# A Mamba block with a ternary feed-forward: stores of products on SyncE, D u on TensorE, the gate on VectorE, and layer-norm sums from ScalarE

## The chip, the cores and the metric

The kernel runs on one core of a Trainium2 chip. The time is device microseconds of one execution. The kernel before takes 3103.6 us (median of 3 runs, 3101.23 to 3104.07). The profiler sees the engines PE (TensorE), DVE (VectorE), ACT (ScalarE), POOL (GpSimd) and SP (SyncE, which only issues DMAs); in the listings, a name with q stands for an engine's queue of instructions that aren't counted as work.

## The reference, cut to what matters

The input x is 4 x 2048 x 256. A Mamba block, then a layer norm of the sum, then a gated feed-forward and another layer norm:

```
x, z   = split(hidden @ in_proj.T)             # 512 channels each
u      = silu(causal_conv4(x) + conv_b)
dt,B,C = split(u @ x_proj.T)                   # 64, 16, 16
delta  = softplus(dt @ dt_proj.T + dt_b)
h_t    = exp(delta_t A) h_{t-1} + (delta_t u_t) B_t     # 512 channels x 16 states
y_t    = sum_n h_t[n] C_t[n] + D u_t
x1     = layernorm(hidden + (y * silu(z)) @ out_proj.T)
f      = silu(s1 * x1 @ W1.T) * (s2 * x1 @ W2.T)        # 1024 wide, ternary weights
f      = gelu(sh1 * f @ H1.T);  f = gelu(sh2 * f @ H2.T)
out    = layernorm(x1 + s3 * f @ W3.T)
```

## The kernel before, in words

The work has two stages. The first runs the Mamba block over 16 tiles of 512 time steps (4 batch rows of 4 tiles), and computes the products W1 x1 and W2 x1 of each tile as well, which it stores to memory (`ab`). The second reads these products and does the rest of the feed-forward. The change touches the first stage; an opening tile without a scan stands ahead of its loop, and a closing part behind it.

**Groups and slots.** A tile has 512 x 16 recurrences of 512 steps. They go through VectorE in 64 groups of 128: 4 channel groups c of 128 channels, in each of them 4 quarters q of the 16 states, in each of these 4 blocks j of 32 channels. One `tensor_tensor_scan` does a group (L1267). Four groups with the same c and q are a step k, 0 to 15. All engines run through the same 64 slots a tile, each engine in its own order, with semaphores between them; in slot i the group n = 20 + i is scanned, so a tile's slots begin with its group 20 and end with group 19 of the next tile. What is done in which slot is written out by hand in tables at the top of the file.

**Who does what.** ScalarE makes exp(delta A) of each group into one of three PSUM banks, two groups ahead (`decay_of`, L908). The scan's other input, db = (delta u) B, comes from VectorE for three quarters (`times_b`, L1251) and from GpSimd for the fourth (L1129). GpSimd multiplies h by C (`times_c`, L1118) into one of two hc buffers. TensorE folds hc over the states into the bank p_y (`fold_step`, L650): four matmuls, one for each block of 32 channels, each with all 128 rows and 32 columns of the array; hc of step k can be written when the fold of k - 2 is done. When a channel group's 4 folds are done, VectorE computes u D + y from u and p_y (`skip`, L1291), and GpSimd multiplies by silu(z) (`gate`, L1146). TensorE then projects and adds the residual, ScalarE copies the four 128-row parts out (L919). For the norm, VectorE takes mean and variance in slots 1 to 5 (`bn_stats`, `bn_aggr`, L1301 and L1306), ScalarE gives a first 1/sqrt in slot 7, GpSimd refines it, ScalarE scales in slot 15.

**delta and its broadcasts.** For each channel group of the next tile, TensorE, ScalarE and VectorE compute the softplus; GpSimd finishes delta and delta u (L1137, L1141). SyncE then runs `copies(t, c)` (L418): it stores delta's rows, stores delta u's rows, waits until these have landed, and loads each of them four times, to the four state rows of 32 partitions: eight loads of 256 KB. SyncE's program per tile was, in this order: copies of group 3, the store of x1, the load of x, copies of the next tile's group 0, the load of xT, copies of groups 1 and 2.

**The products.** Each tile has 16 products e (`AB_PLACES`: slot and bank of each). TensorE makes product e in its slot, ScalarE copies it in the next slot to one of three buffers (`copy_product`, L972), for which the store of product e - 3 has to have landed, and issues the store another slot later (`store`, L957), after waiting for its own copy. After every second product it issues the load of a pair of weights (L951) into a ring of four.

Of the kernel before, what the change touches and what calls it, by code (L numbers as in the profile page):

```python
# [106 lines left out]
SKIP_AFTER, GATE_AFTER = GC - JC + FOLD_AFTER + 1, GC - JC + FOLD_AFTER + 3  # L107
# [3 lines left out]
LN_SLOT = 15  # L111
EXP_LEAD = 2

# [18 lines left out]
GATE_SLOT, FIRST_SLOT = 42, 51  # L132
# [62 lines left out]
def mamba_stage(nc, sems, flag, xT, x, in_wT, conv_w, conv_b, xp_wT, dt_wT, dt_b, A_log, D_param, out_wT,  # L195
                fold, spread, ident, w1T, w2T, h1T, h2T, w3T, scales, d_rows, du_rows, w12, x1, ab):
    ctx = ExitStack()
    with ctx:
# [44 lines left out]
        fold_w = sb("fold_w", [P, GD])  # L243
        taps = sb("taps", [P, KI, TAPS])
        cb = sb("cb", [P, KI])
        dtb = sb("dtb", [P, KI])
        dpar = sb("dpar", [P, KI])
# [3 lines left out]
        stats = sb("stats", [P, SUB, 6])  # L251
        mv = sb("mv", [P, SUB, 2])
        var4, y4, a4, nb4 = (sb(name, [P, SUB]) for name in ("var4", "y4", "a4", "nb4"))
# [62 lines left out]
        y_sb, gated = sem("y_sb"), sem("gated")  # L316
        ln_dve, ln_act, ln_pool, ln_out = sem("ln_dve"), sem("ln_act"), sem("ln_pool"), sem("ln_out")
# [52 lines left out]
        N_NEWTON = 7  # L370
# [14 lines left out]
        kept.stores += [(ab_out[k], PAST.count(ab_uses(k), ab_uses(k) + ABOUT0)) for k in range(ABRING)]  # L385

# [10 lines left out]
        def _(sp):  # L397
            for dst, src in (
                (w_in[:], in_wT.rearrange("(k p) e -> p k e", p=P)),
                (w_xp[:], xp_wT.rearrange("(k p) e -> p k e", p=P)),  # L400
                (w_dt[:], dt_wT),
                (w_out[:], out_wT.rearrange("(k p) e -> p k e", p=P)),
                (taps[:], conv_w.rearrange("(k p) w -> p k w", p=P)),
                (cb[:], conv_b),
                (dtb[:], dt_b),
                (dpar[:], D_param),
                (a_neg[:], A_log),
                (fold_w[:], fold),
                (db[:, 0, 0:2, :].rearrange("p a t -> p (a t)")[DTR:P], spread),
                (db[:, 1, 0, 0:P], ident),  # L410
            ):
                sp.dma_start(dst, src).then_inc(weights_in, 16)
# [5 lines left out]
            def copies(t, c):  # L418

                k = c % 2  # L420
                sp.wait_ge(delta, t.count(KI, c + 1))
                sp.dma_start(d_rows[k], sp_r[k][:]).then_inc(d_out[k], 16)
                sp.wait_ge(du, t.count(KI, c + 1))
                sp.dma_start(du_rows[k], sp_w[k][:]).then_inc(du_out[k], 16)

                sp.wait_ge(db_dve, t.count(KI * QV, QV * (c - 1) + DVE0))
                sp.sem_inc(waited, 1)
                sp.wait_ge(db_pool, t.count(KI, c - 1 + POOL0))
                sp.sem_inc(waited, 1)
                sp.wait_ge(du_out[k], t.count(32, 16 * (c // 2 + 1)))  # L430
                for nn in range(GN):
                    sp.dma_start(du_bc[k][nn * GD:(nn + 1) * GD, :, :],
                                 du_rows[k].rearrange("(j d) t -> d j t", d=GD)).then_inc(du_in[k], 16)

                sp.wait_ge(decay, t.count(NG, GC * (c - 1) + DECAY0))
                sp.sem_inc(waited, 1)
                sp.wait_ge(d_out[k], t.count(32, 16 * (c // 2 + 1)))
                for nn in range(GN):
                    sp.dma_start(d_bc[k][nn * GD:(nn + 1) * GD, :, :],
                                 d_rows[k].rearrange("(j d) t -> d j t", d=GD)).then_inc(d_in[k], 16)  # L440
# [27 lines left out]
            copies(OPENING, 0)  # L468
            load_next(OPENING)
            copies(OPENING, 1)  # L470
            copies(OPENING, 2)

            def tile(t):
                nxt = t.following()
                rows = slice(t.tt * NT, (t.tt + 1) * NT)
                if t is LAST_ROW[-1]:
                    closing_loads(t)
                copies(t, 3)
                store_x1(t)
# [5 lines left out]
                sp.dma_start(res[:], x[t.b, rows, :].rearrange("(s p) c -> p s c", p=P)).then_inc(x_in, 16)  # L485
                if exists(nxt):
                    copies(nxt, 0)
                if exists(nxt.following()):
                    load_next(nxt)
                if exists(nxt):  # L490
                    copies(nxt, 1)
                    copies(nxt, 2)
# [16 lines left out]
            def closing(t):  # L509
                for m in range(KH):  # L510
# [9 lines left out]
                sp.wait_ge(first_lo, KH)  # L520
                for j in range(RAW_PLACES + EARLY_POOL_PIECES):
# [10 lines left out]
            closing(LAST_ROW[-1])  # L532
# [3 lines left out]
        def _(pe):  # L536
# [268 lines left out]
        def _(act):  # L805
# [111 lines left out]
            def residual(t, s):  # L917
                act.wait_ge(out_mm, t.count(SUB, s + 1))
                act.activation(res[:, s, :], p_mm[s % 2][:, 0:DM], ACT.Copy).then_inc(out_sb, 1)  # L919

            def norm(t, i):
                if i == 7:
                    act.wait_ge(ln_dve, t.count(2 * SUB, 2 * SUB))
                    act.activation(var4[:], mv[:, :, 1:2].rearrange("p a b -> p (a b)"), ACT.Ln,
                                   bias=eps_col[:]).then_inc(ln_act, 1)
                    act.wait_ge(ln_act, t.count(2, 1))
# [23 lines left out]
            def load_w12(t, m):  # L950
                act.dma_start(w12_sb[m % W12RING][:].bitcast(F32), w12[m]).then_inc(w12_in[m % W12RING], 16)  # L951

            def store(t, e):
                at = (ab[0:TILES].rearrange("(b q) e p t -> b q e p t", q=TILES_B)[t.b, t.tt, e] if exists(t)
                      else ab[TILES, e])
                act.wait_ge(ab_sb, ab_done(t, e + 1))
                act.dma_start(at, ab_sbuf[e % ABRING][:]).then_inc(ab_out[e % ABRING], 16)  # L957

# [9 lines left out]
            def copy_product(t, e):  # L968
# [5 lines left out]
                m = e // 2 + W12RING  # L974
                if e % 2 == 1 and m < KH:
                    load_w12(t, m)
                elif e % 2 == 1 and exists(t):
                    load_w12(t.following(), m - KH)

# [6 lines left out]

            def ffn_stores(t, i):
                for e in range(AB):
                    if i == AB_PLACES[e][0] + 2:
                        store(t, e)  # L990
# [43 lines left out]
            def closing():  # L1034
                ffn_stores(PAST, 0)
                norm(PAST, LN_SLOT - 8)
# [11 lines left out]
                for e in range(AB):  # L1048
# [3 lines left out]
                    store(PAST, e)  # L1052
# [4 lines left out]
            def tile(t):  # L1057
                nxt = t.following()
                for i in range(NG):
# [3 lines left out]
                    if t is BEFORE and i == W12_FIRST:  # L1063
                        act.wait_ge(w12_out, 16 * 2 * KM)
                        for m in range(W12RING):
                            load_w12(OPENING, m)
                    if exists(t):
                        ffn_stores(t, i)
# [23 lines left out]
                if exists(t):  # L1092
                    ffn_stores(t, NG)
# [9 lines left out]
        def _(pool):  # L1103
# [4 lines left out]
            pool.sem_inc(gated, GATED0)  # L1108
# [34 lines left out]
            def gate(t, c):  # L1143
                pool.wait_ge(y_sb, t.count(KI, c + 1 + 1))
                pool.wait_ge(silu_z, t.count(1, 1))
                pool.tensor_tensor(z_of(t, c), u_of(t, c), z_of(t, c), ALU.mult).then_inc(gated, 1)  # L1146

            def norm(t):
# [5 lines left out]
                var = mv[:, :, 1:2].rearrange("p a b -> p (a b)")  # L1154
                mean = mv[:, :, 0:1].rearrange("p a b -> p (a b)")
                pool.wait_ge(ln_act, t.count(2, 2))
                pool.sem_inc(waited, 1)
                pool.tensor_scalar(var4[:], var, EPS, 1.0, ALU.add, ALU.mult).then_inc(ln_pool, 1)
# [8 lines left out]
                pool.tensor_tensor(nb4[:], mean, y4[:], ALU.mult).then_inc(ln_pool, 1)  # L1167
                done(6)
                pool.tensor_scalar(nb4[:], nb4[:], -1.0, 0.0, ALU.mult, ALU.add).then_inc(ln_pool, 1)

            def tile(t):
                nxt = t.following()
                for i in range(NG):
# [17 lines left out]
                    if n % GC == GATE_AFTER % GC:  # L1191
                        now, g = at_group(t, n - GATE_AFTER)
                        if exists(now):
                            gate(now, g // GC)
# [32 lines left out]
        def _(dve):  # L1227
# [4 lines left out]
            for j in range(KI):  # L1232
                for k in range(TAPS):
# [5 lines left out]
            dve.memset(res[:], 0.0).then_inc(out_sb, OUT0)  # L1239
# [3 lines left out]
            dve.sem_inc(y_sb, 1)  # L1243
# [50 lines left out]
            STATS_SLOT, AGGR_SLOT = 1, 5  # L1294

            def norm(t, i):
                if STATS_SLOT <= i < STATS_SLOT + SUB:
                    s = i - STATS_SLOT
                    if s == 0:
                        dve.wait_ge(out_sb, t.count(SUB, OUT0))  # L1300
                    dve.bn_stats(stats[:, s, :], res[:, s, :]).then_inc(ln_dve, 1)  # L1301
                elif i == AGGR_SLOT:
# [804 lines left out]
```

## Time and profile before

| what | us |
|---|---|
| median of 3 runs | 3103.6 |
| profiled execution | 3103.3 |
| its span, first to last instruction | 3101.5 |
| DVE busy | 2338.7 (75%) |
| PE busy | 2724.2 (88%) |
| ACT busy | 2010.8 (65%) |
| POOL busy | 1784.3 (58%) |
| one tile of the scan, the tenth of 16 | 117.7 |

The page gives the busy time of each engine over the span, and in 40 slices of it, about 78 us each. A group of instructions is printed with its line, engine, operation, result and operands, count, busy time and the mean duration of one, then the idle time of its engine just ahead of it and what ended that. A timeline row gives the start, the duration, the engine, the line and the operation, and in brackets the idle time ahead of it with its releaser. Durations of neighbours overlap a little, since instructions are pipelined; where it matters, differences of starts are taken.

### The profile page before, as it was taken

The page shows a single profiled execution, that of the slowest core. Times are in us where ns is not written, and L with a number is a line of the kernel's source. Part 1 is how long each engine was busy: PE and PEld are TensorE (multiplying, and loading weights), DVE is VectorE, ACT ScalarE, POOL GpSimd, SP SyncE. Part 2 cuts the span into 40 slices and gives each one's busy share as a digit, 9 for nine tenths or more (in the row PEclk, how much of TensorE's full clock was granted, in tenths as well). Part 3 has the DMA queues.
Part 4 walks back from the last instruction along what each step waited for, and adds up shares of the span by engine and source line. Part 5 has one row for each costly group of instructions (what it writes and reads, how often), then busy time and mean ns, then how long its engine had stood idle before and what let it go on. Part 6 is the DMA issues. An engine that isn't in the chain of part 4 may idle for free. (4 is left out here: it accounts for less than half of the span.)

```text
span 3101.5 us, 39954 instructions
## 1 busy us (share of the span) xinstructions
PE 2724.2 (88%) x11028; PEld 1636.8 (53%) x11028; DVE 2338.7 (75%) x2781; ACT 2010.8 (65%) x3383; POOL 1784.3 (58%) x920
## 2 busy tenths in 40 slices
PE   5788988888888888888888876889999999999997
PEld 2243443343343333333333332678888888888886
DVE  5999999999999999999999999434444454444442
ACT  3777777777777777777777777555555445555442
POOL 3899999899899899999999999400000000000000
PEclk8888898989889889889889887899999999999999
DMA  7366466466475475564565566542222222222210
GB/s 254 93 189 166 121 192 163 117 190 164 118 194 149 131 197 134 145 195 127 155 183 130 164 166 192 199 159 87 83 68 88 74 68 87 89 68 83 80 41 15
DMA packets 239642, 411.98 MB, mean 133 GB/s; under 512 B 23264, under 2 KB 63456, under 8 KB 239456
## 3 DMA queue, kind: packets, MB, share of 16 engines
q1 hardware_dynamic: 175680, 297.67, 35.3%
q10 hardware_dynamic: 63776, 112.22, 11.2%
q8 instruction: 69, 1.13, 0.2%
q14 instruction: 117, 0.96, 0.1%
HBM read 285.55 MB, written 124.26 MB: 132 GB/s over the span
## 5 line engine op out<-in xcount | busy, mean ns | idle before, releaser
L1267 DVE TENSOR_TENSOR_SCAN h<-bank,state,db 128x512 f32<-128x512 f32 x1024 | 1252.5, 1266 | 70.9 <-ACT bank L908 37.5
L1118 POOL TENSOR_TENSOR hc<-h,c_rows 128x1024 f32<-128x1024 f32 x512 | 1202.0, 2378 | 15.3 <-DVE h L1267 10.4
L908 ACT ACTIVATE bank<-d_bc,a_neg 128x512 f32<-128x512 f32 x1024 | 692.8, 685 | 314.5 <-DVE h L1267 201.9
L1627 ACT ACTIVATE hring<-s_bank,sc 128x512 f32<-128x512 f32 x248 | 170.5, 688 | 488.9 <-PE s_bank L1560 488.5
L1560 PE MATMUL s_bank<-mid,h_r 128*128 128x512 f32 x2048 | 469.1, 390 | 4.6 <-DVEq L1654 4.6
L722 PE MATMUL bank<-x_t,w 128*128 128x512 f32 x1088 | 394.1, 492 | 55.8 <-ACT ab L972 46.9
L1251 DVE TENSOR_TENSOR db<-bank,du_bc 128x2048 f32<-128x2048 f32 x192 | 435.1, 2266 | 8.1 <-issue 7.8
L1560 PEld LDWEIGHTS s_bank<-mid,h_r 128*128 128x128 f32 x2048 | 385.8, 188 | 85.6 <-ACTq L1598 5.0
L1129 POOL TENSOR_TENSOR db<-du_bc,b_row 128x2048 f32<-128x2048 f32 x64 | 291.7, 4558 | 102.4 <-DVE h L1267 97.7
L629 PE MATMUL bank<-bc,w_spread 64*128 64x512 f32 x272 | 155.6, 581 | 217.7 <-DVE db L1251 214.5
L650 PE MATMUL bank<-hc,fold_w 128*32 128x512 f32 x2048 | 334.6, 731 | 8.6 <-DVE u L1291 5.0
L722 PEld LDWEIGHTS bank<-x_t,w 128*128 128x128 f32 x1088 | 220.4, 217 | 215.4 <-issue 102.7
L629 PEld LDWEIGHTS bank<-bc,w_spread 64*128 64x128 f32 x272 | 58.0, 215 | 396.4 <-DVE db L1251 275.8
L582 PE MATMUL bank<-xb,w_conv 128*128 128x512 f32 x512 | 254.2, 626 | 13.4 <-ACT uz L829 9.5
L972 ACT ACTIVATE ab<-bank 128x512 f32<-128x512 f32 x272 | 160.1, 588 | 122.3 <-PE bank L722 107.7
L1560 PE MATMUL s_bank<-s_end,h_r 128*128 128x512 f32 x1024 | 235.7, 391 | 0.0
L1685 DVE TENSOR_TENSOR mid<-hring,mid 128x512 fp32r<-128x512 f32 x120 | 81.5, 690 | 177.7 <-ACT mid L1630 177.7
L1560 PEld LDWEIGHTS s_bank<-s_end,h_r 128*128 128x128 f32 x1024 | 191.8, 188 | 41.4
L582 PEld LDWEIGHTS bank<-xb,w_conv 128*128 128x128 f32 x512 | 90.0, 192 | 162.8 <-issue 142.9
L1560 PE MATMUL s_bank<-first_lo,h_r 128*128 128x512 f32 x448 | 175.4, 391 | 0.0
L1560 PE MATMUL s_bank<-first_hi,h_r 128*128 128x512 f32 x448 | 175.3, 391 | 0.0
L1685 DVE TENSOR_TENSOR first_lo<-hring,first_hi 128x512 fp32r<-128x512 f32 x64 | 44.3, 692 | 147.3 <-ACT first_hi L1630 147.3
(143 smaller groups left out, 3698.1 us busy)
## 6 DMA issues: line engine op xcount, KB each, us to landing
ab<-ab ACTq DMA_DIRECT2D x272, 256.0 KB, 4.1
du_bc<-du_rows SPq DMA_DIRECT2D x256, 256.0 KB, 4.9
d_bc<-d_rows SPq DMA_DIRECT2D x256, 256.0 KB, 7.9
s_abr<-ab SPq DMA_DIRECT2D x120, 512.0 KB, 3.9
w<-w ACTq DMA_DIRECT2D x136, 256.0 KB, 3.9
d_rows<-sp_r SPq DMA_DIRECT2D x64, 256.0 KB, 2.0
du_rows<-sp_w SPq DMA_DIRECT2D x64, 256.0 KB, 2.0
x<-res SPq DMA_DIRECT2D x17, 512.0 KB, 8.9
```

Of the source, the lines that this page charges most:

```text
L582: last = pe.matmul(p_mm[j % 2][:], w_conv[:, c, k, :], xb[:, c, k:k + NT], start=k == 0, stop=k == TAPS - 1)
L629: pe.matmul(dst[:], spread_w[:, which, :], bc[t.tt % 2][DTR:P, :], start=True, stop=True).then_inc(done, 1)
L650: last = pe.matmul(p_y[GD * j:GD * j + GD, :], fold_w[:], hc[:, k % HCSTEPS, j, :], start=q == 0, stop=q == QN - 1, tile_position=(0, GD * j))
L722: last = pe.matmul(product_bank(t, e)[:], w12_sb[m % W12RING][:, which, k, :], x_t[j][:, k, :], start=k == 0 and j == 0, stop=k == KM - 1 ...
L908: act.activation(decays[DECAY_BANK[g]][:], d_bc[c % 2][:, j, :], ACT.Exp, scale=a_neg[:, g:g + 1]).then_inc(decay, 1)
L972: act.activation(ab_sbuf[e % ABRING][:], product_bank(t, e)[:], ACT.Copy, scale=-1.0).then_inc(ab_sb, 1)
L1118: pool.tensor_tensor(hc[:, k % HCSTEPS, at:at + HG], h[:, H_SLOT[k], at:at + HG], c_rows[:, q, :].unsqueeze(1).broadcast_to([P, HG, NT]), ...
L1129: pool.tensor_tensor(db[:, k % DBSTEPS], du_bc[c % 2][:], b_row[:].unsqueeze(1).broadcast_to([P, JC, NT]), ALU.mult).then_inc(db_pool, 1)
L1251: dve.tensor_tensor(db[:, k % DBSTEPS], p_b[:].unsqueeze(1).broadcast_to([P, JC, NT]), du_bc[c % 2][:], ALU.mult).then_inc(db_dve, 1)
L1267: dve.tensor_tensor_scan(h[:, H_SLOT[k], j, :], decays[DECAY_BANK[g]][:], db[:, k % DBSTEPS, j, :], state[:, g:g + 1], ALU.mult, ALU.add). ...
L1560: last = pe.matmul(p_h[m % HBANKS][:], hidden_weights(layer, k, m), ins[j][:, k, :], start=k == 0 and j == 0, stop=k == KH - 1 and j == pa ...
L1627: act.activation(hring[c % RING][:], p_h[m % HBANKS][:], ACT.Gelu, scale=sc[:, 2 + layer, m:m + 1]).then_inc(gelu, 1)
```

## The change

It has four parts, and what goes with them.

1. Mean and variance: ScalarE's copy of the residual sum (L919) also accumulates its sum; in slot 1 ScalarE makes the negative mean, in slots 2 to 5 the squares of the differences with an accumulated sum, in slot 7 the first 1/sqrt from these. VectorE's `bn_stats` and `bn_aggr` go. GpSimd's refinement has one small operation less.
2. The gate: VectorE multiplies p_y by silu(z) straight from PSUM, in the slot where `skip` stood. GpSimd's gate goes.
3. D u: a matrix w_skip (the fold matrix with rows scaled by D, made once) multiplies u on TensorE into p_y, four matmuls of 32 x 32 in front of one of the folds of each channel group: step 3 of group 0, 2 of group 1, 1 of groups 2 and 3.
4. The stores of the products and the loads of weights: SyncE issues them, in slots. Its whole program is put in slots for that: the four steps of `copies` in the slots 6 to 9 after that group's `DT_SLOTS`, the store of x1 in slot 17, the load of x in 23, of xT in 34, some loads of the closing part in 25, 29 and 38.

```diff
+GATE_AFTER = GC - JC + FOLD_AFTER + 1
+SKIP_STEP = (3, 2, 1, 1)
+COPY_AFTER, COPY_STEPS = 6, 4
+STORE_SLOT, X_SLOT, XT_SLOT = 17, 23, 34
...
+            def products(t, i):
+                for e in range(AB):
+                    if i == AB_PLACES[e][0] + 2:
+                        store(sp, t, e)
+                        m = e // 2 + W12RING
+                        if e % 2 == 1 and m < KH:
+                            load_w12(sp, t, m)
+                        elif e % 2 == 1 and exists(t):
+                            load_w12(sp, t.following(), m - KH)
...
+                for i in range(NG):
+                    if t is LAST_ROW[-1]:
+                        first_loads(t, i)
+                    products(t, i)
+                    for step in range(COPY_STEPS):
+                        for now, c in dt_places(t, i, COPY_AFTER + step):
+                            if exists(now):
+                                copies(now, c, step)
+                    if i == STORE_SLOT:
+                        store_x1(t)
+                    elif i == X_SLOT:
+                        load_x(t)
+                    elif i == XT_SLOT and exists(nxt.following()):
+                        load_next(nxt)
...
                 if q == 0:
-                    pe.wait_ge(y_sb, t.count(KI, c + 1))
+                    pe.wait_ge(gated, t.count(KI, c + GATED0))
+                if q == SKIP_STEP[c]:
+                    for j in range(JC):
+                        at = slice(GD * j, GD * j + GD)
+                        pe.matmul(p_y[at, :], w_skip[at, c, :], u_of(t, c)[at, :], start=False, stop=False,
+                                  tile_position=(GD * j, GD * j))
                 pe.wait_ge(hc_done, t.count(TURNS * NK, TURNS * (k + 1) + HC0))
...
-                act.activation(res[:, s, :], p_mm[s % 2][:, 0:DM], ACT.Copy).then_inc(out_sb, 1)
+                act.activation(res[:, s, :], p_mm[s % 2][:, 0:DM], ACT.Copy,
+                               accum_out=sums[:, s:s + 1]).then_inc(out_sb, 1)
...
+                if i == MEAN_SLOT:
+                    act.wait_ge(out_sb, t.count(SUB, OUT0))
+                    act.activation(mean4[:], sums[:], ACT.Copy, scale=-1.0 / DM).then_inc(ln_act, 1)
+                elif MEAN_SLOT < i <= MEAN_SLOT + SUB:
...
+                    act.activation(sp_e[:, s % 2 * DM:(s % 2 + 1) * DM], res[:, s, :], ACT.Square, bias=mean4[:, s:s + 1],
+                                   accum_out=squares[:, s:s + 1]).then_inc(ln_act, 1)
...
-            def skip(t, c):
-                u = u_of(t, c)
+            def gate(t, c):
                 dve.wait_ge(folded, t.count(NK, QN * (c + 1) + FOLDED0))
-                dve.scalar_tensor_tensor(out=u, in0=u, scalar=dpar[:, c:c + 1], in1=p_y[:],
-                                         op0=ALU.mult, op1=ALU.add).then_inc(y_sb, 1)
+                dve.wait_ge(silu_z, t.count(1, 1))
+                dve.tensor_tensor(z_of(t, c), p_y[:], z_of(t, c), ALU.mult).then_inc(gated, 1)
```

## Rows read from the trace of the kernel before

**Rows 1.** The page: VectorE's busy share in 40 slices, in tenths.
```profile
DVE  5999999999999999999999999434444454444442
```
**Rows 2.** Windows, one tile: length, busy per engine (instructions), granted clock, DMA share, GB/s.
```profile
1136.25:1253.97 117.72, 100.20 (x363) 44.64 (x363) 112.41 (x99) 88.78 (x157) 108.75 (x56) 0.89 0.59 157
```
**Rows 3.** Waits over the whole span: us in total, times, longest.
```profile
ACT bank L908 <- ACT ab L972: 87.0, 149, 0.9
...
DVE h L1267 <- ACT bank L908: 37.5, 49, 2.9
DVE h L1267 <- POOL hc L1118: 29.4, 19, 2.0
```
**Rows 4.** Groups by line: count, busy us, mean ns, idle ahead and its releaser.
```profile
L1146 POOL TENSOR_TENSOR uz<-uz 128x512 f32<-128x512 f32 x48 | 62.0, 1292 | 9.4 <-DVE uz L1291 9.4
L1291 DVE SCALAR_TENSOR_TENSOR uz<-uz,dpar,bank 128x512 f32<-128x512 f32 x48 | 35.3, 734 | 4.9 <-PE bank L650 4.3
L1301 DVE BATCH_NORM_STATS2 stats<-res 128x6 f32<-128x256 f32 x68 | 27.7, 411 | 16.3 <-ACT res L919 16.3
L1285 DVE TENSOR_TENSOR bc<-bank,bc 32x512 fp32r<-32x512 f32 x16 | 11.0, 691 | 0.7
```
**Rows 5.** Timeline of VectorE, slots 0 to 5 of a tile.
```profile
1058.85 0.42 DVE L1301 BATCH_NORM_STATS2 stats<-res 128x6 f32<-128x256 f32 x1
1059.18 1.27 DVE L1267 TENSOR_TENSOR_SCAN h<-bank,state,db 128x512 f32<-128x512 f32 x1
...
1061.38 1.28 DVE L1267 TENSOR_TENSOR_SCAN h<-bank,state,db 128x512 f32<-128x512 f32 x1 [0.61 <-ACT bank L908]
...
1066.24 0.35 DVE L1306 BATCH_NORM_AGGREGATE mv<-stats 128x2 f32<-128x6 f32 x4
1066.51 1.25 DVE L1267 TENSOR_TENSOR_SCAN h<-bank,state,db 128x512 f32<-128x512 f32 x1
```
**Rows 6.** Timeline of TensorE: fold 13 in slot 42, granted clock low.
```profile
1016.62 1.94 PE L650 MATMUL bank<-hc,fold_w 128*32 128x512 f32 x8
```
**Rows 7.** Timeline of GpSimd: times_c 15, behind fold 13.
```profile
1018.75 4.71 POOL L1118 TENSOR_TENSOR hc<-h,c_rows 128x1024 f32<-128x1024 f32 x2 [0.20 <-PE bank L650]
```
**Rows 8.** Timeline of SyncE: the copies of group 1.
```profile
1026.07 0.33 SPq L424 DMA_DIRECT2D du_rows<-sp_w  x1
1028.09 1.87 SPq L432 DMA_DIRECT2D du_bc<-du_rows  x4
1030.14 2.12 SPq L439 DMA_DIRECT2D d_bc<-d_rows  x4
```
**Rows 9.** DMA issues at 1062.6: the last of eight copies, KB, us to landing.
```profile
d_bc<-d_rows SPq DMA_DIRECT2D x1, 256.0 KB, 8.4
```
**Rows 10.** DMA issues from 1031.0 to 1031.2, amid the copies of group 1.
```profile
d_bc<-d_rows SPq DMA_DIRECT2D x1, 256.0 KB, 8.7
ab<-ab ACTq DMA_DIRECT2D x1, 256.0 KB, 8.8
```
**Rows 11.** Timeline of ScalarE: copy of product 14 in slot 53, decay of slot 56.
```profile
1037.29 0.58 ACT L972 ACTIVATE ab<-bank 128x512 f32<-128x512 f32 x1
...
1038.77 0.69 ACT L908 ACTIVATE bank<-d_bc,a_neg 128x512 f32<-128x512 f32 x1 [0.90 <-DVE h L1267]
```
**Rows 12.** Timeline of VectorE: the scans of slots 40 and 56.
```profile
1010.38 1.28 DVE L1267 TENSOR_TENSOR_SCAN h<-bank,state,db 128x512 f32<-128x512 f32 x1 [1.80 <-POOL hc L1118]
...
1039.76 1.28 DVE L1267 TENSOR_TENSOR_SCAN h<-bank,state,db 128x512 f32<-128x512 f32 x1 [1.03 <-POOL hc L1118]
```
**Rows 13.** Timeline of TensorE at full clock: one product in two passes; a fold.
```profile
1089.61 1.02 PE L596 MATMUL bank<-uz,w_xp 128*96 128x512 f32 x2
1090.56 1.06 PE L650 MATMUL bank<-hc,fold_w 128*32 128x512 f32 x8
```
**Rows 14.** Timeline of SyncE and ScalarE: copies of group 0, copy of product 5.
```profile
1113.38 1.74 SPq L432 DMA_DIRECT2D du_bc<-du_rows  x4
...
1121.99 0.58 ACT L972 ACTIVATE ab<-bank 128x512 f32<-128x512 f32 x1
```

More of the change, by code:

```diff
@@ L385, in mamba_stage, with load_w12, store @@
         kept.stores += [(ab_out[k], PAST.count(ab_uses(k), ab_uses(k) + ABOUT0)) for k in range(ABRING)]
+        def load_w12(eng, t, m):
+            if m >= W12RING or not is_first(t):
+                eng.wait_ge(ab_sb, ab_done(t, 2 * (m - W12RING) + 2))
+            eng.dma_start(w12_sb[m % W12RING][:].bitcast(F32), w12[m]).then_inc(w12_in[m % W12RING], 16)
+        def store(eng, t, e):
+            at = (ab[0:TILES].rearrange("(b q) e p t -> b q e p t", q=TILES_B)[t.b, t.tt, e] if exists(t)
+                  else ab[TILES, e])
+            eng.wait_ge(ab_sb, ab_done(t, e + 1))
+            eng.dma_start(at, ab_sbuf[e % ABRING][:]).then_inc(ab_out[e % ABRING], 16)
         block = ctx.enter_context(nc.Block())
@@ L416, in load_xT, with copies @@
                              .rearrange("(k p) t -> p k t", p=P)).then_inc(xT_in, 16)
-            def copies(t, c):
+            def copies(t, c, step):
                 k = c % 2
[L421 to L440, printed above, removed]
@@ new lines, in copies @@
+                if step == 0:
+                    sp.wait_ge(delta, t.count(KI, c + 1))
+                    sp.dma_start(d_rows[k], sp_r[k][:]).then_inc(d_out[k], 16)
+                elif step == 1:
+                    sp.wait_ge(du, t.count(KI, c + 1))
+                    sp.dma_start(du_rows[k], sp_w[k][:]).then_inc(du_out[k], 16)
+                elif step == 2:
+                    sp.wait_ge(db_dve, t.count(KI * QV, QV * (c - 1) + DVE0))
+                    sp.sem_inc(waited, 1)
+                    sp.wait_ge(db_pool, t.count(KI, c - 1 + POOL0))
+                    sp.sem_inc(waited, 1)
+                    sp.wait_ge(du_out[k], t.count(32, 16 * (c // 2 + 1)))
+                    for nn in range(GN):
+                        sp.dma_start(du_bc[k][nn * GD:(nn + 1) * GD, :, :],
+                                     du_rows[k].rearrange("(j d) t -> d j t", d=GD)).then_inc(du_in[k], 16)
+                else:
+                    sp.wait_ge(decay, t.count(NG, GC * (c - 1) + DECAY0))
+                    sp.sem_inc(waited, 1)
+                    sp.wait_ge(d_out[k], t.count(32, 16 * (c // 2 + 1)))
+                    for nn in range(GN):
+                        sp.dma_start(d_bc[k][nn * GD:(nn + 1) * GD, :, :],
+                                     d_rows[k].rearrange("(j d) t -> d j t", d=GD)).then_inc(d_in[k], 16)
@@ L467, in _, with load_x @@
             sp.wait_ge(checked, 8)
[L468 to L479, printed above, removed]
+            for c in range(KI - 1):
+                for step in range(COPY_STEPS):
+                    copies(OPENING, c, step)
+                if c == 0:
+                    load_next(OPENING)
+            def load_x(t):
                 sp.wait_ge(x1_out, t.count(16, 16))
@@ L484, in tile @@
                 sp.sem_inc(waited, 1)
[L485 to L492, printed above, removed]
+                sp.dma_start(res[:], x[t.b, t.tt * NT:(t.tt + 1) * NT, :].rearrange("(s p) c -> p s c", p=P))\
+                  .then_inc(x_in, 16)
+            def tile(t):
+                nxt = t.following()
+                if t is LAST_ROW[-1]:
+                    closing_loads(t)
+                for i in range(NG):
+                    if t is LAST_ROW[-1]:
+                        first_loads(t, i)
+                    products(t, i)
+                    for step in range(COPY_STEPS):
+                        for now, c in dt_places(t, i, COPY_AFTER + step):
[7 more added lines that the diff above has]
+                        load_next(nxt)
             def load_pool(j):
@@ L507, in closing_loads, with first_loads @@
                     load_piece(sp, raw[j][:], j).then_inc(raw_h1_in[j], 16)
-            def closing(t):
-                for m in range(KH):
+            def first_loads(t, i):
+                for m in FIRST_LOADS.get(i, ()):
                     if m == 2:
@@ L1034, in closing @@
             def closing():
-                ffn_stores(PAST, 0)
-                norm(PAST, LN_SLOT - 8)
+                for i in range(8):
+                    norm(PAST, i)
                 norm(PAST, LN_SLOT)
@@ L1051, in closing @@
                     copy_product(PAST, e)
-                    store(PAST, e)
+                    store(act, PAST, e)
+                    m = e // 2 + W12RING
+                    if e % 2 == 1 and m < KH:
+                        load_w12(act, PAST, m)
             for i in range(X_SLOTS[0], X_SLOTS[-1] + 2):
@@ L1166, in norm @@
                 done(5)
[L1167 to L1169 removed]
+                pool.tensor_tensor(nb4[:], mean4[:], y4[:], ALU.mult).then_inc(ln_pool, 1)
             def tile(t):
@@ L1286, in low_rows @@
                                   rows[DTR:DTR + 2 * NS, :].bitcast(F32), ALU.subtract).then_inc(xd_lo, 1)
-            def skip(t, c):
-                u = u_of(t, c)
+            def gate(t, c):
                 dve.wait_ge(folded, t.count(NK, QN * (c + 1) + FOLDED0))
-                dve.scalar_tensor_tensor(out=u, in0=u, scalar=dpar[:, c:c + 1], in1=p_y[:],
-                                         op0=ALU.mult, op1=ALU.add).then_inc(y_sb, 1)
[L1294 to L1302, printed above, removed]
-                    dve.wait_ge(ln_dve, t.count(2 * SUB, SUB))
-                    dve.sem_inc(waited, 1)
-                    for s in range(SUB):
-                        dve.bn_aggr(mv[:, s, :], stats[:, s, :]).then_inc(ln_dve, 1)
+                dve.wait_ge(silu_z, t.count(1, 1))
+                dve.tensor_tensor(z_of(t, c), p_y[:], z_of(t, c), ALU.mult).then_inc(gated, 1)
             def not_rounded(piece, raw, rounded):
@@ L1370, in tile @@
                         low_rows(nxt)
-                    if n % GC == SKIP_AFTER % GC:
-                        now, g = at_group(t, n - SKIP_AFTER)
+                    if n % GC == GATE_AFTER % GC:
+                        now, g = at_group(t, n - GATE_AFTER)
                         if exists(now):
-                            skip(now, g // GC)
+                            gate(now, g // GC)
                     if t is LAST_ROW[-1]:
@@ L1389, in _ @@
                 tile(t)
-            for i in range(AGGR_SLOT + 1):
-                norm(PAST, i)
             dve.wait_ge(counted, 1)
```

97 lines of the change are left out of this document (38 added, 59 removed).

## The prediction

> **What bounds the kernel now.** First the page's busy slices [rows 1]: the span has two parts. Over the first 26 of 40 slices, the Mamba scan, VectorE reads 9 throughout; then the feed-forward part, which the change doesn't touch, follows. So the question is what one tile of the scan costs. The windows view from one tile's first group to the next [rows 2] gives 117.7 us a tile, of it VectorE 112.4, GpSimd 108.8, TensorE 100.2, ScalarE 88.8. VectorE sets the pace, and some 5 us a tile are waits of VectorE. The waits view names them [rows 3]: its scans wait 37.5 us in all for ScalarE's decays and 29.4 us for GpSimd; and ScalarE itself loses 87 us of idle ahead of decays behind its own copies of products: it waits for a copy to end, issues the store, and only then goes on. So what VectorE sheds is worth its full time, and what makes a decay late is paid in full as soon as it exceeds these small waits.
>
> **Part 1: statistics leave VectorE.** In the first five slots of a tile stand four bn_stats and four bn_aggr. From start to start [rows 5] a bn_stats costs 1059.18 - 1058.85 = 0.33, the aggregates 1066.51 - 1066.24 = 0.27: 4 x 0.33 + 0.27 = 1.6 us a tile (the mean of 0.41 in [rows 4] counts an overlap with the scan). Two of the four lie ahead of a scan that waits 0.61 for a decay after the large silu; that gain holds only if ScalarE comes as much earlier there, and it does: its last store before that silu goes away (next part). In exchange ScalarE gets a mean and four squares of 256 columns in slots 1 to 5, and accumulators on its four copies of the projection. They hide behind the scans: a decay goes to one of three banks and waits for the scan three groups back, so ScalarE has idle time there once it has caught up. If that cover were gone, each would delay a decay by its own length, about the 0.41 of the bn_stats [rows 4], 2 us a tile. I take 0. After the last tile ScalarE does for the last norm what VectorE did, the same number of passes over the same columns: 0.
>
> **Part 2: the gate.** skip (0.73, [rows 4]) becomes the gate on VectorE, one tensor_tensor with an operand in PSUM; nearest row 0.69. 4 x 0.04 = 0.16 a tile gained. GpSimd's four gates of 1.29 go; it is not the engine that VectorE waits for most, and its wait ahead of slot 40 (1.80, [rows 12]) is made by times_b and times_c after scan 55, which stay. Parts 1 and 2: 1.75 x 16 tiles = 28 us less.
>
> **Part 3: D u on TensorE.** Per channel group four matmuls on 32 x 32 blocks of the array, 512 columns. The nearest row is the fold, four column blocks side by side: eight passes in 1.06 at full clock [rows 13], 1.94 at half clock [rows 6]; the granted clock is at its lower level around slot 42, after TensorE waited for VectorE. Lower bound 0 (TensorE idles there anyway), upper bound one after another: one 512-column product of two passes is 1.02 [rows 13], so 4.1 at full and 8.1 at half clock. I take the fold's own price, 1.9 at half clock: same shape of output, same columns. In three of the groups TensorE waits for VectorE soon after, and the 1.9 disappears. In the fourth it does not: the skip of group 3 stands right ahead of fold 13. Fold 13 frees the hc buffer for which GpSimd's times_c 15 waits now already (0.20, [rows 7]); behind times_c 15 GpSimd does delta and du of the next tile's group 1, and these release SyncE's copies. So those copies go out 1.9 us later.
>
> By the Trainium skill's page "TensorEngine Tiling (Array Packing)", section "Restrictions and Gotchas", different row tiles cannot access the same PSUM bank at one time. The four blocks here are different row tiles that all write p_y. The fold of the trace has column blocks only, so no row here shows which holds; by the rule the price would be the upper bound above, and that is rival C.
>
> **Part 4: the stores on SyncE.** ScalarE gets back its issue waits (87.0 / 149 = 0.58 a store, [rows 3]), which removes the two waits of VectorE at slots 54 and 56. But SyncE issues in one order, slot by slot: steps 2 and 3 of the copies of group 1 stand at slots 46 and 47, the store of product 11 at slot 48. Now ScalarE issues that store beside them. The path in one tile, from VectorE's slot 40 at 1010.38 [rows 12]:
> - du's rows are stored at 1026.07 and the eight broadcast copies begin when they have landed, at 1028.09 [rows 8]. New: 1028.09 + 1.9 = 1030.0.
> - SyncE needs 1030.14 + 2.12 - 1028.09 = 4.2 us to issue them; the store of product 11 comes behind, at about 1034.
> - Transfers land in the order of their issue, whatever queue: a store that ScalarE issued at 1031.06 amid such copies took 8.8 us, the copy beside it on SyncE 8.7 [rows 10]. Eight undisturbed copies: the last, issued 3.2 to 3.6 after the first, takes 8.4 [rows 9], so all are there 11.7 after the first issue; with 2 us of latency (1026.07 to 1028.09) that is 1.2 for each 256 KB. The store lands at 1030.0 + 11.7 + 1.2 = 1042.9.
> - The ring of products has three buffers. The copy of product 14 (now at 1037.29, [rows 11]) needs the buffer of product 11, so it waits until 1042.9. Behind it on ScalarE's queue is the decay of slot 56: 1042.9 + 0.58 + 0.69 [rows 11] + 0.1 = 1044.3, where VectorE scans at 1039.76 today [rows 12].
> That is +4.55 us a tile, the wait of 1.03 that goes already counted. The bounds: with a hidden skip 1.9 less, +2.65; if the store were in time, -1.5 (the waits at slots 54 and 56, the first of which comes from the same store issues). TensorE and GpSimd wait meanwhile and catch up; nothing on VectorE later than slot 56 waits on a clock of its own, so the delay stays.
>
> The same happens at group 0, milder: there the copies begin at 1113.38, the store of product 2 comes behind them, and the copy of product 5 stands at 1121.99 [rows 14]. At the old time it would land at 1113.4 + 11.7 + 1.2 = 1126.3, 4.3 late. GpSimd, without the two gates ahead of that delta (2 x 1.29, [rows 4]) and on a VectorE that comes 0.6 earlier, brings the copies forward by 2.0: 2.3 late. Of that 1.8 falls into VectorE's wait at slot 40 [rows 12]. I count +0.5 a tile, and against it 0.5 for the waits that VectorE has at a tile's end that the last store's issue causes: 0. What else SyncE now does in that order costs 0: the loads of w12 fill a ring of four, two products ahead of need; the store of product 0 stands behind the load of x, which waits for x1 to land, but its buffer is wanted eight slots later; the load of xT moves to slot 34 and is wanted at slot 47.
>
> **The sum.** 15 tiles have copies for a next tile. In two of them TensorE runs at full clock at slot 42, and the delay is about 3.5; 13 x 4.55 + 2 x 3.5 = 66. With the 28 gained: +38 us. Against the profiled execution, 3103.3 (its span 3101.5 and 1.8 around it), that is 3141; the median of the runs is 3103.6, the same within 0.01%. I say 3140.
>
> **The rivals.**
> A, faster: product 11 lands before 1037 and there is no wait. It decides at a landing within 3 us of its issue at 1034. For it: a store with nothing ahead of it lands in 2 us [rows 8]. Against it: [rows 10]. Then VectorE gains 28, and up to 1.0 a tile at slots 54 and 56, 15: 3103 - 43 = 3060. Chance 0.17.
> B, about the same: TensorE hides the skip (full clock, or its wait for VectorE at slot 45 takes it up before GpSimd notices). 15 x 2.65 - 28 = +12: 3115. For it: the bound of GpSimd is only 0.20 wide [rows 7]. Against it: the clock there is low in 13 of 15 tiles. Chance 0.13.
> C, slower still: the four blocks run one after another. 6.2 more in the path of slot 42 a tile: 15 x 10.7 - 28 = +133, and delays at slots 14 and 26 on top: 3236 and more. Against it: the fold's blocks run side by side. Chance 0.08.
> D, slower: at group 0 GpSimd is not earlier, and of the 4.3 only 1.8 are covered: 15 x 2.5 = 37 more, 3177. For it: GpSimd is within 4% of VectorE [rows 2]. Against it: the two gates are real work. Chance 0.12.
> The forecast, 3118 to 3165, has 0.50.
>
> **The numbers.** No change means within 0.2%, 6 us, about what can be told from the runs. Faster: A and 0.03 of B, 0.20. The same: 0.06 of B and 0.04 of the forecast's low edge, 0.10. Slower: the rest, 0.70. The range leaves out most of A (below 3085) and C: 3085 to 3190. The forecast's own range is 3118 to 3165.
>
> **What would show it.** Right: in the waits, ScalarE's copies of products wait for ab stores by some 60 us or more (a few us now), in slot 53 of each tile, and VectorE's scans wait longest for ScalarE's decays; a tile is near 120 us; bn_stats is gone and the gate is near 0.69; the skip's passes are near the fold's. Wrong: if a store issued behind eight copies lands in under 5 us, or product 14's copy is not held, the path of part 4 fails and the kernel is faster; if the skip's four blocks are far apart in time, it is C.

## The result, and the profile after

The changed kernel takes 3179.0 us (median of 4 runs, 3166.7 to 3192.1) where the kernel before takes 3103.8 on the same chip: ratio 1.0245, with a 95% interval of 1.0202 to 1.0287. The forecast was 3140. The direction held and the time lies inside the outer range of 3085 to 3190, but above the forecast's own range, 3118 to 3165: the loss of 75 us is twice the 37 forecast. The profiled execution is the longest of the four: 3192.1 us, its span 3190.3, 88.8 more than the span before. From the end of the last scan on both kernels take the same (1148.3 us, 1147.8 before), so all of it lies in the scan's stage.

Windows of two tiles of the changed kernel, columns as in [rows 2]:
```profile
1189.44:1308.37 118.93, 102.30 (x396) 44.11 (x395) 110.33 (x90) 89.86 (x171) 103.82 (x51) 0.93 0.58 155
569.10:695.27 126.17, 108.07 (x399) 46.81 (x395) 110.46 (x91) 89.43 (x171) 103.80 (x50) 0.88 0.54 147
```
VectorE's work fell from 112.41 to 110.4 a tile, GpSimd's from 108.75 to 103.8, and yet a tile is longer. There are two kinds of tiles now, of 119 to 122 and of 124 to 127 us, the long ones at a lower granted clock.

The waits over the whole span, which answer to [rows 3]:
```profile
ACT ab L1032 <- DMA ab<-ab: 164.9, 34, 8.6
POOL hc L1165 <- PE bank L706: 154.1, 45, 8.0
...
DVE h L1303 <- ACT bank L964: 140.8, 75, 7.1
...
PE bank L778 <- ACT ab L1032: 102.9, 37, 6.1
```
The same two waits for stores and for folds in the kernel before:
```profile
ACT ab L972 <- DMA ab<-ab: 9.6, 7, 2.5
...
POOL hc L1118 <- PE bank L650: 2.6, 9, 1.0
```
Of the changed kernel's lines the first and the third are the forecast's: ScalarE's copies wait for stores, and VectorE's scans for the decays behind these copies. The second is new: GpSimd's times_c waits 154 us for folds. Nothing in the prediction has it.

SyncE's timeline at the copies of group 0, against [rows 14], then at those of group 1, against [rows 8]; both in the same tile:
```profile
1158.86 0.34 SPq L405 DMA_DIRECT2D ab<-ab  x1
1159.25 0.45 SPq L399 DMA_DIRECT2D w<-w  x1
1159.75 0.43 SPq L446 DMA_DIRECT2D du_rows<-sp_w  x1
1163.20 1.74 SPq L455 DMA_DIRECT2D du_bc<-du_rows  x4
1165.13 1.73 SPq L463 DMA_DIRECT2D d_bc<-d_rows  x4
1167.12 0.97 SPq L405 DMA_DIRECT2D ab<-ab  x2
...
1196.40 0.32 SPq L446 DMA_DIRECT2D du_rows<-sp_w  x1
...
1198.47 1.74 SPq L455 DMA_DIRECT2D du_bc<-du_rows  x4
1200.39 1.73 SPq L463 DMA_DIRECT2D d_bc<-d_rows  x4
1202.40 0.36 SPq L405 DMA_DIRECT2D ab<-ab  x1
```
The stores of product 2 (1167.12) and of product 11 (1202.40) stand behind eight copies each. The first took this long from issue to landing (the second 8.3), against [rows 10]:
```profile
ab<-ab SPq DMA_DIRECT2D x1, 256.0 KB, 9.1
```
The copy issued just ahead of it took 9.3. So on SyncE's queue, too, the store landed when the copies ahead of it had. What it does downstream, first on ScalarE (copies of products 5 and 14, against [rows 11]):
```profile
1176.31 0.60 ACT L1032 ACTIVATE ab<-bank 128x512 f32<-128x512 f32 x1 [5.21 <-DMA ab<-ab]
...
1210.76 0.60 ACT L1032 ACTIVATE ab<-bank 128x512 f32<-128x512 f32 x1 [3.82 <-DMA ab<-ab]
```
and then on VectorE (slots 38, 40 and 56, against [rows 12]):
```profile
1177.61 2.46 DVE L1303 TENSOR_TENSOR_SCAN h<-bank,state,db 128x512 f32<-128x512 f32 x2 [3.48 <-ACT bank L964]
1180.62 1.28 DVE L1303 TENSOR_TENSOR_SCAN h<-bank,state,db 128x512 f32<-128x512 f32 x1 [0.56 <-POOL hc L1165]
...
1212.24 1.28 DVE L1303 TENSOR_TENSOR_SCAN h<-bank,state,db 128x512 f32<-128x512 f32 x1 [3.60 <-ACT bank L964]
```
That is a short tile. TensorE waits for the copy of product 5 before it can make product 6:
```profile
1176.96 2.08 PE L778 MATMUL bank<-x_t,w 128*128 128x512 f32 x4 [5.27 <-ACT ab L1032]
```
In a long tile TensorE comes late between the two stalls. Its granted clock from product 6 (behind the copy of product 5) to fold 13, in the short tile and in a long one (busy, clock, DMA share, GB/s):
```profile
1176.96:1188.80 11.84, 11.04 (x44) 0.85 0.41 141
554.14:570.98 16.84, 15.79 (x44) 0.54 0.40 144
```
The wait is 5.3 us in the short tile and 4.5 in the long one. Behind it TensorE runs at the lower of its two levels (1.2 and 2.4 GHz), for a few us in the one tile, over almost the whole stretch in the other. The same 44 matmuls end 5 us later, and GpSimd's times_c 15, which releases delta and the copies of group 1, shows it:
```profile
571.32 4.73 POOL L1165 TENSOR_TENSOR hc<-h,c_rows 128x1024 f32<-128x1024 f32 x2 [7.66 <-PE bank L706]
```
In this execution 7 of 15 tiles are long. In another one (3168.5 us) there were 4. At some 5 us a long tile, that is most of the 23.6 us between these two.

VectorE's gate by line, against `skip` of [rows 4]:
```profile
L1327 DVE TENSOR_TENSOR uz<-bank,uz 128x512 f32<-128x512 f32 x64 | 43.2, 675 | 1.6 <-PE bank L706 1.1
```

### The profile page after: what moved, and what is told of

Its sections match the earlier page's. It is cut to its first block and busy times, and to the rows that moved or that the text cites. A ratio compares the mean times of both kernels' runs of the same rounds, so it can differ in the third digit from the quotient of the medians.

```text
span 3190.3 us, 41089 instructions
## 1 busy us (share of the span) xinstructions
PE 2791.1 (87%) x11540; PEld 1648.6 (52%) x11540; DVE 2305.7 (72%) x2650; ACT 2030.7 (64%) x3600; POOL 1700.8 (53%) x839
## 5 line engine op out<-in xcount | busy, mean ns | idle before, releaser
L706 PE MATMUL bank<-hc,fold_w 128*32 128x512 f32 x2048 | 309.8, 681 | 5.9 <-DVE uz L1327 5.3
L679 PE MATMUL bank<-bc,w_spread 64*128 64x512 f32 x272 | 144.1, 541 | 177.4 <-DVE db L1287 177.4
```

Source lines behind the costliest of these rows:

```text
L679: pe.matmul(dst[:], spread_w[:, which, :], bc[t.tt % 2][DTR:P, :], start=True, stop=True).then_inc(done, 1)
L706: last = pe.matmul(p_y[GD * j:GD * j + GD, :], fold_w[:], hc[:, k % HCSTEPS, j, :], start=q == 0, stop=q == QN - 1, tile_position=(0, GD * j))
```

## The experiments

Times are medians; the kernel before had 3102 to 3105 beside them. **S** is the theory that the loss is two stores behind eight copies.

**Stores on ScalarE again.**
```diff
-                    products(t, i)
...
+                    if exists(t):
+                        ffn_stores(t, i)
```


> The changed kernel, but ScalarE issues the stores of the products and the loads of weights again, as before; SyncE's copies keep their new slots. Theory S (two stores wait behind the eight broadcast copies of groups 0 and 1): both stalls are gone, only parts 1 to 3 are left, 3103 - 28 = 3075 us (3065 to 3085), no wait of ScalarE's copies for ab stores over 20 us in all, and no wait of times_c for a fold. Rival T (the skip on TensorE, or the norm's passes on ScalarE, make the loss): the waits of times_c for folds stay, and the time stays above 3130.


Measured 3080.1 (ratio 0.9929, 0.9906 to 0.9951). Its waits:
```profile
POOL hc L1176 <- PE bank L705: 62.8, 31, 3.8
...
ACT ab L1031 <- DMA ab<-ab: 5.6, 6, 2.1
```
Parts 1 to 3, with SyncE's other work in slots, gain 24.6, the forecast's 28 nearly. The wait for stores is gone. That for folds is not, which S had wrong, but VectorE's scans wait no longer for GpSimd than before (23.6 us in all, 29.4 before). Moving the issue to SyncE makes the loss: 3179 - 3080 = 99.

**Copies behind the stores.** SyncE keeps all issues; only steps 2 and 3 of the copies of groups 0 and 1 (the loads, four in each step) move in its order.
```diff
-COPY_AFTER, COPY_STEPS = 6, 4
+COPY_PLACES, COPY_STEPS = ((6, 7, 10, 12), (6, 7, 10, 11), (6, 7, 8, 9), (6, 7, 8, 9)), 4
```


> The changed kernel, SyncE still issues everything, but steps 2 and 3 of the copies of group 0 stand behind the stores of products 2 and 3 (slots 30 and 32), those of group 1 behind the store of product 11 (slots 48 and 49). Theory S: both stalls go; ScalarE also keeps its gain from not issuing, so 3055 to 3080 us. Rival Q (a store issued by SyncE is late in itself, because one queue issues everything in turn): ScalarE still waits for ab stores by 80 us or more and the time is above 3120. Rival T: above 3130.


Measured 3059.0 (0.9854, 0.9831 to 0.9877). Its waits:
```profile
POOL hc L1166 <- PE bank L707: 51.5, 26, 4.6
...
ACT ab L1033 <- DMA ab<-ab: 10.6, 8, 3.8
```
So the order alone costs 120 us, and with the stores in time it is 21 better that SyncE issues them than that ScalarE does. This is rival A's state, and its 3060.

**One group at a time.** The same edit with (6, 7, 8, 9) kept for group 1, then for group 0.


> Only group 0's copies moved behind the stores of products 2 and 3; product 11 still behind eight copies. Theory S, with the group 0 stall as the cause of the long low clock of TensorE and so of the late fold 13 in some tiles: left is 15 x 3.1 us at slot 56, 3075 + 47 = 3122 us (3105 to 3130), delta of group 1 13 to 14 us after slot 40 in every tile, tiles all of one length. If the late fold 13 comes from the skip instead: some tiles still 5 us longer, 3140 or more.

> Only group 1's copies moved behind the store of product 11; product 2 still behind eight copies of group 0. Theory S: the stall at slot 38 and its sequel at slot 42 stay, some 3.3 us a tile or 50 us in all, the one at slot 56 goes: 3075 + 50 = 3125 us, up to 3150 where the late fold 13 of some tiles still makes group 1's decays late. If group 0's stall were taken up by GpSimd's slack at slot 40, as I had counted: 3075 to 3085.


Measured 3165.5 with group 1's stall alone, which no theory had, and 3118.5 with group 0's alone, as S. Against 3059 the stalls are worth 106 and 60, together 120: they overlap. My 47 for group 1 was too small since I took the 3.1 us by which slot 56 of a short tile is later than in the kernel before; without any stall that slot comes 1.5 earlier than before, and with group 0's stall gone TensorE is at its lower level at fold 13 in nearly all tiles. ScalarE's copy of product 14 with group 1's stall alone, and VectorE's scan behind it:
```profile
1305.79 0.60 ACT L1033 ACTIVATE ab<-bank 128x512 f32<-128x512 f32 x1 [6.72 <-DMA ab<-ab]
```
```profile
1307.27 1.28 DVE L1304 TENSOR_TENSOR_SCAN h<-bank,state,db 128x512 f32<-128x512 f32 x1 [6.01 <-ACT bank L965]
```
From slot 40 (1273.65) to that scan it is 33.6 us; the prediction had 1044.3 - 1010.38 = 33.9. In these tiles GpSimd begins delta of group 1 13.5 to 15 after slot 40; with group 0's stall alone 9 of 15 have it at 17 to 18.5. So the long tiles are a sequel of group 0's stall.

**Part 4 alone.** The kernel before with SyncE's program of the changed one.


> The kernel before with SyncE's new program alone: it issues the stores and the loads of weights in the changed kernel's slots; statistics, gate and D u stay where they were. Theory S: the loss lies here alone, and parts 1 to 3 only hide 24 us of it (3080 with them and ScalarE's stores, against 3105 before): 3179 + 24 = 3203 us (3185 to 3220), with ScalarE's copies of products 5 and 14 waiting for stores as in the changed kernel. Rival T (the new operations make part of the loss): well under that, 3150 or less.


Measured 3250.3 (1.0473, 1.0441 to 1.0504): part 4 by itself makes the loss, as S has it, but the loss is 146, above S's range, and parts 1 to 3 give back 71 of it, not 24. Delta of group 0 comes 1.6 us later than in the changed kernel (GpSimd still has the gates; that these make it was not tried by itself), its copies begin 15 to 17 us after slot 24 in place of 14, the copy of product 5 follows, and ScalarE waits longer:
```profile
ACT ab L1008 <- DMA ab<-ab: 191.1, 33, 7.9
```

**Part 1 alone.**


> The kernel before with the mean and variance from ScalarE's sums alone. By the forecast's count 1.6 x 16 = 26 us less than before, 3078, so that parts 2 and 3 with SyncE's other slots are worth 0 beside it (3080 was measured with all). If the squares on ScalarE delay decays in slots 2 to 5, 0.4 each: 3090 or more, and parts 2 and 3 give the rest.


Measured 3092.0, 12.5 less: half of the count. That is the time of the expectation's second reading, but not its reason: the scans of slots 3 to 7 wait for nothing. VectorE's timeline, slot 2, against the 0.61 of [rows 5]:
```profile
938.26 2.46 DVE L1277 TENSOR_TENSOR_SCAN h<-bank,state,db 128x512 f32<-128x512 f32 x2 [1.38 <-ACT bank L907]
```
VectorE loses 1.5 us of work a tile and gains 1.1 of waits, 0.7 of it here: the two bn_stats that stood ahead of this scan were cover. The prediction's condition, that ScalarE comes earlier there, does not hold while ScalarE issues the stores: the scans of slot 2 wait 20.9 us in all here and 21.1 with parts 1 to 3 and the stores on ScalarE, but 13.8 with SyncE issuing in time (9.5 before). The other 12 of the 24.6 were not taken apart.

**The skip's price.** In the kernel with group 1's stall, D u is left out.
```diff
-                    for j in range(JC):
+                    for j in range(0):
                         at = slice(GD * j, GD * j + GD)
                         pe.matmul(p_y[at, :], w_skip[at, c, :], ...
```


> The kernel with group 0's copies reordered (3165 us) without the matmuls of D u, which are left out of y. The forecast put the skip at 1.9 us at half clock in the path fold 13, times_c 15, delta, copies, store of product 11, copy 14, slot 56. If that holds: 15 x 1.0 to 1.9 less, 3137 to 3150. If TensorE's idle time hides the skip, or the copies wait for something else: 3160 to 3168.


Measured 3099.7, 66 less. TensorE with and without the skip, ahead of fold 13 at the lower level:
```profile
1279.89 1.93 PE L703 MATMUL bank<-uz,w_skip 32*32 32x512 f32 x8
1281.76 1.70 PE L707 MATMUL bank<-hc,fold_w 128*32 128x512 f32 x8
```
```profile
1248.59 2.07 PE L779 MATMUL bank<-x_t,w 128*128 128x512 f32 x4
1250.59 1.46 PE L707 MATMUL bank<-hc,fold_w 128*32 128x512 f32 x8
```
The skip takes 1.87, the 1.9 of the forecast, and slot 56 moves by 1.9 (31.6 after slot 40 in place of 33.6, over 15 tiles). As much again comes between slot 56 and the next tile's slot 24 (1.5 a tile), where VectorE's waits of slots 0 and 2 fall from 33 to 10 us in all; the forecast had put the skips of the other groups, which stand there, at nothing. Which of them makes it was not tried.

> The kernel with both groups reordered (3059 us) without the matmuls of D u, which are left out of y. In the kernel with group 1's stall the same removal gave 66 us. Theory P (the skip costs what the path through fold 13 and the copies makes of it): with no copy of a product waiting for a store, 0 to 10 us less, 3049 to 3059. Rival T (the skip costs by itself, wherever it stands): again some 60 less, about 3000.


Measured 3079.6: 21 us slower than with the skip; both theories miss. Windows from slot 44 to 52 of one tile, with the skip and without (columns as in [rows 2]):
```profile
1227.41:1241.81 14.40, 12.98 (x52) 6.20 (x49) 14.40 (x13) 10.77 (x23) 12.30 (x7) 1.00 0.54 162
```
```profile
1239.28:1254.77 15.49, 13.18 (x40) 5.94 (x41) 14.50 (x12) 10.19 (x21) 12.47 (x7) 0.78 0.57 169
```
With less to do TensorE is granted less (0.78 for 1.00) and needs longer for fewer matmuls. VectorE's gate at the end of that stretch then waits for the fold, 12.7 us in 15 tiles, and not at all with the skip:
```profile
1254.16 0.69 DVE L1328 TENSOR_TENSOR uz<-bank,uz 128x512 f32<-128x512 f32 x1 [0.99 <-PE bank L707]
```
The stretch from slot 40 to 56 is 1.3 longer a tile, 19 of the 21.

**TensorE kept busy in its wait.** The changed kernel, with extra matmuls whose result nobody reads; BUSY is 10 in the first run and 5 in the second.
```diff
+                if e == 6 and exists(t):
+                    pe.wait_ge(gated, t.count(KI, KI - 1 + GATED0))
+                    for _ in range(BUSY):
+                        pe.matmul(p_y[:], w_out[:, 0, 0:P], w_out[:, 0:2, :].rearrange(...), start=True, stop=True)
```


> The changed kernel (3179 us) with ten extra matmuls into p_y in each tile, ahead of TensorE's wait for the copy of product 5, at a time when p_y is free: 4 us of work in a wait of 5. Theory K (after that wait TensorE is granted its lower clock, for long in some tiles, and fold 13 is late for that): the clock stays up, no delta of group 1 later than 15 us after slot 40, tiles of one length near 120, 3145 to 3165. Rival B (fold 13 is late from the backlog of that wait alone): unchanged or later, 3175 to 3190.

> The changed kernel with five extra matmuls into p_y ahead of TensorE's wait for the copy of product 5, in place of ten: ten took 8.85 us there, 4 more than the wait, and the scan of slot 40 waited for that, 68 us in all against 8. Five take 4.4, inside the wait. Theory K (late fold 13 comes from the granted clock after that wait): tiles of one length near 120, no delta of group 1 later than 15 us after slot 40, the wait at slot 40 small again, 3145 to 3165. Rival B: two lengths of tiles as in the changed kernel, 3175 to 3190.

> The changed kernel itself beside the run above, on the same chip: 3165 to 3192 us, in steps of some 5 us for each tile with a late fold 13.


With ten: 3188.5, in B's range, but not for B's reason: all tiles are of one length (121 to 125) and delta of group 1 begins 12 to 13 after slot 40 in every tile, as K has it, while the extra work outlasts the wait. With five: 3123.7, beside 3169.6 for the changed kernel itself (3158 to 3188), 46 less. The stretch that was at 0.85 and 0.54 above, from product 6 to fold 13 (columns as in [rows 2]):
```profile
1139.50:1151.00 11.50, 10.16 (x46) 4.19 (x46) 10.11 (x9) 10.04 (x20) 9.03 (x5) 1.00 0.46 156
```
No tile is long any more (117 to 121). That is theory K, and more than its 3145 to 3165, since the short tiles also had a stretch at the lower level.

**The last tile.**
```diff
-FIRST_LOADS = {25: (0, 1), 29: (2, 3, 4, 5), 38: (6, 7)}
+FIRST_LOADS = {32: (0,), 33: (1,), 34: (2,), 35: (3,), 36: (4,), 37: (5,), 38: (6,), 39: (7,)}
...
-                    elif i == X_SLOT:
+                    elif i == (33 if t is LAST_ROW[-1] else X_SLOT):
```


> The kernel with both groups reordered (3059 us), and in the last tile the load of x after the store of product 3 (slot 33 in place of 23) and the eight loads of the next stage one a slot from slot 32 on. Its last tile took 37.9 us from slot 24 to the last scan against 33.8 before, with product 2's store issued 4.5 us later. Theory S (again stores behind something on SyncE's queue): 4 us less, 3055. If the last tile is held by the loads' traffic and not by the order: no difference.


Measured 3053.6 (0.9833, 0.9815 to 0.9851), 5.4 less, near S's 4; but in the profiles the last tile itself gives only 1.9 of that. The rest lies where nothing was changed, so it is not shown to be the edit's. It is the fastest version: 51 us below the kernel before.

## Why the prediction was wrong

The mechanism of part 4 was right, and group 1 came near its price; **the step that failed is group 0: "I count +0.5 a tile, and against it 0.5 ...: 0"**. The runs show +1.74 a tile there, 26 us, and a sequel in the next stretch that the sum does not have; as the only stall it costs 60 (3118.5 against 3059.0). By differences of scan starts, means over 15 tiles, profiled execution against profiled execution; the last column but one is the execution with 4 long tiles, and the forecast's 0 of group 0 stands as its two halves, 0.5 x 15 each, in the stretches where they belong:

| stretch | before | after | change x 15 | with 4 long tiles | forecast |
|---|---|---|---|---|---|
| slot 24 to 40 (group 0's stall) | 29.23 | 30.97 | +26 | +26 | +8 |
| slot 40 to 56 (group 1's) | 29.08 | 34.45 | +81 | +66 | +66 |
| slot 56 to 24 of the next tile | 59.11 | 57.53 | -24 | -33 | -34 |
| opening, last tile, closing | | | +6 | +6 | -2 |

Group 0's term is not the whole of it. Without that stall alone the kernel still takes 3165.5, not 3140. In its profile the first two stretches are then -3 and +67, but the third gains only 15 in place of 34; with D u left out as well it gains 38. So the skips that were put at nothing ("the 1.9 disappears") have a price in that kernel.

- **Parts 1 and 2**, -28: -24.6 with the stores on ScalarE. VectorE's work fell by 2.0 a tile, a little more than the 1.75 counted; bn_stats and bn_aggr are gone, the gate takes 0.675. Part 1 by itself loses half of its gain to the wait of slot 2.
- **Part 3**: the price of 1.9 at the lower level is right in the path of fold 13; for the other groups see above. Rival C is out. By the Trainium skill's page "TensorEngine Tiling (Array Packing)", section "Restrictions and Gotchas", different row tiles cannot access one PSUM bank at one time. Here four 32 x 32 blocks at four row tiles write p_y in 1.87 us, the time of the fold's column blocks at that level (1.94, [rows 6]), so the trace does not show that price.
- **Part 4, group 1**: copies at 1030.0, product 11's store issued at about 1034, landed at 1042.9, slot 56 at 1044.3; with this stall alone, counted from slot 40, they came 19.9, 23.8, 32.1 and 33.6 after it, where the forecast had 19.6, 23.6, 32.5 and 33.9. In the changed kernel the short tiles are earlier (31.6 to 33.0) since TensorE is back at full clock at fold 13, and the seven long ones later (35.4 to 37.6). In the execution with 4 long tiles the sum was the forecast's, +66: short tiles below its price and long ones above it, so that this agreement is partly luck.
- **Part 4, group 0**: delta came 1.8 earlier (means over 15 tiles), near the 2.0 counted. But the copies began only 0.6 earlier, because the store of du's rows now stands behind a store of a product and a load of weights: the copies begin 1163.20 - 1159.75 = 3.45 after it (3.6 in the mean, 2.2 with the stores on ScalarE), not 1113.38 - 1111.35 = 2.03 as here:
```profile
1111.35 0.34 SPq L424 DMA_DIRECT2D du_rows<-sp_w  x1
```
The store of product 2 then landed 12 to 13 us after the first copy, as forecast (11.7 + 1.2), and the copy of product 5 was 4.1 late, not 2.3. VectorE's wait at slot 40 took up 1.3 of that. Rival D, group 0 fully late, gave 3177, 2 us from the result; that is luck, since its reason (GpSimd no earlier) did not hold and it had +37 where 26 were measured.
- **What no case had**: the wait of TensorE for that copy, its lower clock behind it and so the late fold 13; and the last tile, 4.4 longer, whose stores stand behind the load of x and the next stage's loads (1.9 came back when these were moved).
- **The order of landing**: by the Trainium skill's page "DMA: Bandwidth & Descriptors", section "Issuing engines are not separate DMA queues", transfers run on the same 16 engines whichever engine issues them. The traces agree: 8.8 us for a store amid copies from ScalarE [rows 10], 9.1 behind them from SyncE. What the change altered was the place in the order.

Open is what decides in a tile whether TensorE's lower clock lasts a few us or 15; the same program had 7 long tiles in one execution and 4 in another.

## What to carry to other kernels

When DMA issues move to another engine's queue, write down for each what it is now issued behind, and compare the landing of that with the next use of its buffer; putting the stores that were wanted soon ahead of the copies turned 3179 into 3059. A wait that is off the critical path can still cost if the engine that waits is TensorE: look at the granted clock behind the wait, not only at its length. And two stalls in one loop need not be additive (106 and 60 alone, 120 together): measure each with the other removed.

## What the runs showed of the hardware

- More matmuls made the kernel faster, twice: 3123.7 against 3169.6 with five of no use a tile, 3059.0 against 3079.6 with the skip, each time with the granted clock at 1.00 in the stretches shown, in place of 0.54 to 0.85. Ten, which outlast the wait, gave 3188.5, no gain. By the Trainium skill's page "TensorE: Matmul & The Clock Gate", section "Loop structure matters more than you think", a long wait for a DMA ahead of the matmuls makes them run cold. The trace agrees, with a wait of 5 us for ScalarE in place of a DMA (0.85 and 0.54 behind it).
- A ScalarE pass with an accumulated sum is two instructions: 0.50 for 256 columns and 0.19 for reading the accumulator. From the groups by line of the kernel with part 1 alone:
```profile
L933 ACT ACTIVATE sp_e<-res,mean 128x256 f32<-128x256 f32 x68 | 33.9, 499 | 0.0
L933 ACT ACTIVATION_READ_ACCUMULATOR sp_e<-res,mean 128x1 f32 x68 | 13.1, 192 | 0.0
```
